# Four edits to the state-space layer of a four-layer kernel on one core

## The chip, the cores and the metric

## The reference

The input is x, 8 sequences of 512 tokens with 256 features. The change touches the third layer alone:

```python
xp = x @ Wx.T                       # 512 columns: 64 heads of 8
Bm = rmsnorm((x @ WB.T).reshape(B_, L, H, N), Bn_w) + B_bias     # H = 64, N = 128
Cm = rmsnorm((x @ WC.T).reshape(B_, L, H, N), Cn_w) + C_bias
dt = softplus(x @ Wdt.T);  lam = sigmoid(x @ Wlam.T)
theta_cumsum = cumsum((x @ Wth.T).reshape(B_, L, H, N // 2) * dt[..., None], axis=1)
Bm, Cm = rope(Bm, theta_cumsum), rope(Cm, theta_cumsum)
alpha = exp(-dt * exp(A_log));  beta = (1 - lam) * dt * alpha;  gamma = lam * dt
# over the tokens, per head:
h = alpha * h + beta * outer(B_prev, x_prev) + gamma * outer(B, x)
y = C @ h
```

with x normalised before it, and `y * silu(z) @ Wout.T` behind it.

## The kernel before, in words

Each layer is a row of phases; a phase is a function with a block of its own, in which the five queues (SP for transfers, TensorE, ScalarE, VectorE, GpSimd) run lists written out by hand and wait for each other on counted semaphores. A barrier parts the phases. Products in full precision are done as three fp32r matmuls over a high and a low part (`matmul3`, L45; its lines L48 to L50), for each of two blocks of 128 features, so a 128x512 product is six matmuls.

Three phases matter here. `gates` (L870) computes dt, lam and the decays: TensorE's eight products `ga_z`, ScalarE's Sigmoid, Abs, Exp, Ln (L946 to L952), a long row of 128x2048 operations on VectorE, two more Exp (L954 on `tmp`, L956 for the growths), and twelve groups of transpositions whose copies (L962) go to DRAM as `token_gates`. `input_projection` (L1003) computes xp in 32 tiles of 128 tokens: six matmuls, a copy by ScalarE (L1065), a store by SP (L1025); VectorE first copies each tile's x_hi and x_lo into a staging buffer.

`state_space` (L1182) is the long one. Its work is 256 turns, 32 pairs of heads times 8 sequences, two turns (j = 0, 1) to a loop iteration. A turn takes a sequence of 512 tokens as four chunks (TPB) of 128 tokens. Within a chunk the recurrence is a masked product (scores times decay), between chunks it is a state carried by sums. Turn k projects, normalises and rotates B and C of unit k, while scores, sums and outputs are made for the units before it. TensorE's list (`turn`, L1497) is:

- half of B (`p_b[1]`), the angle of the next unit (into `p_sum`), `outputs` (L1432 over the states, L1438 over the masked scores), the other half of B, `exponents` (L1447, L1449: decay exponents into the score banks `p_se`)
- half of C, `turn_b` e = 0 (three transpositions, L1461, into `p_c[0]`, and the growth rows spread by four small matmuls, L1464), `squares` 0 (the sum of B's squares over a head, L1495, into `p_sum`, which the angle has just left), the other half of C
- `turn_b` e = 1 into `p_m`, `scores` (L1476), `chunk_sums` (L1485: `bt`, 128 columns, is the loaded side, `xe`, 16 columns, the moving one), `squares` 1 (the sum of C's squares)

ScalarE squares the projections (L1573, L1580), takes exponents (`decays`, L1553), copies the transposed B (L1559), makes 1/sqrt as Ln and Exp (L1564, L1566) and the sines (`angles`, L1545 to L1549). Ln and Exp need another function table than Sin, so each turn has two table loads. VectorE runs `phases` (L1607 to L1612: dt times angle, running sum, fraction `fr`), `combine` (L1616, L1617), `rotate` for B (L1624 to L1629), `states` with `masked` (L1634 to L1646) and `rotate` for C. GpSimd adds squares and halves of the rotation, splits the next weights (L1380, L1382), adds the diagonal to the decays (L1363, L1367) and scales xp (L1394, L1396). SP loads, per turn, one weight chunk, the growth and decay rows (`load_rows`) and dt rows spread over 64 partitions each (`load_dt`, L1259).

What orders a turn around the change, on TensorE:

```python
def squares(k, q):
    pe.wait_ge((ss_b, ss_c)[q], k + 1)
    if q == 0:
        pe.wait_ge(fr_done, k + 2)
    else:
        pe.wait_ge(ln_b, k + 1)
    M(p_sum[:], pairs_sum[:], sq[:, q, 0], start=True, stop=True).then_inc((sum_b, sum_c)[q], 1)
```

## Time and profile before

| | |
|---|---|
| median of 3 runs | 6169.8 us (6169.16 to 6174.46) |
| the profiled execution | 6162.61 us, its span 6160.8 us |
| TensorE busy | 5549.1 us (90%) |
| VectorE busy | 4509.5 us (73%) |
| GpSimd busy | 3636.6 us (59%) |
| ScalarE busy | 3505.7 us (57%) |
| mean granted tensor clock | 0.945 |

Busy times are shares of the whole span; the phases have different limits, so they are only a first look. A timeline row gives the start, the duration, the engine, the line, the tiles written and read, the count of merged instructions, and in brackets the idle time before it with what ended it. TensorE's durations run until a matmul's last result is out, so they overlap; what a group costs TensorE is read from its start to the next group's start.

### The profile page before, as it was taken

To read this page: it belongs to the slowest core of one execution; us is meant where nothing else is said; L and a number is where in the kernel's file an instruction comes from. 1 tells how busy PE (TensorE), PEld (TensorE's weight loads), DVE (VectorE), ACT (ScalarE), POOL (GpSimd) and SP (SyncE) were. 2 spreads that over 40 slices of the span, in tenths; PEclk is the share of its full clock that TensorE was granted. 3 is DMA by queue.
4 is the path that set the end of the run, shared out by engine and by line. 5 is a ranking of instruction groups with operands and counts; after the bars stand their busy time and mean duration, and the time that the engine had idled before them with its cause. 6 is when DMAs were issued, how large, how long until landed. Compare 5 with 4: busy or idle time off the path is not lost. (4 is left out here: it accounts for less than half of the span.)

```text
span 6160.8 us, 127971 instructions
## 1 busy us (share of the span) xinstructions
PE 5549.1 (90%) x40796; PEld 3972.6 (64%) x40796; DVE 4509.5 (73%) x6856; ACT 3505.7 (57%) x4756; POOL 3636.6 (59%) x4101
## 2 busy tenths in 40 slices
PE   5999588459999999999999999999999999984699
PEld 3454277337777777777777777777777777763587
DVE  5777555538888888888888888888888888835444
ACT  2444222227777777777777777777777777731222
POOL 2222000018888888888888888888888888820000
PEclk9889599679999999999999999999999999986799
DMA  3333200131111111111111111111111111121100
GB/s 100 108 114 118 79 18 24 38 121 32 29 29 30 28 34 29 29 29 30 32 28 31 29 32 29 29 31 27 34 29 29 29 30 32 28 90 62 42 24 20
DMA packets 435078, 267.89 MB, mean 43 GB/s; under 512 B 269092, under 2 KB 363876, under 8 KB 434052
## 3 DMA queue, kind: packets, MB, share of 16 engines
q1 hardware_dynamic: 417284, 257.14, 15.1%
q10 hardware_dynamic: 17664, 9.44, 0.5%
q14 instruction: 101, 0.83, 0.0%
q8 instruction: 29, 0.48, 0.0%
HBM read 186.73 MB, written 66.85 MB: 41 GB/s over the span
## 5 line engine op out<-in xcount | busy, mean ns | idle before, releaser
L1564 ACT ACTIVATE ss_r<-ss_pssum,ss_eps 128x512 f32<-128x512 f32 x512 | 352.9, 689 | 901.8 <-PE ss_pssum L1495 901.8
L1624 DVE SCALAR_TENSOR_TENSOR ss_psb<-ss_psb,ss_norm,ss_r 128x512 f32<-128x512 f32 x512 | 362.9, 754 | 446.4 <-ACT ss_r L1566 446.4
L1495 PE MATMUL ss_pssum<-ss_sq,ss_pairssum 128*128 128x512 f32 x1024 | 570.9, 639 | 57.7 <-DVE ss_fr L1612 57.7
L1376 POOL TENSOR_TENSOR ss_sq<-ss_sq 128x512 f32<-128x512 f32 x256 | 329.6, 1287 | 451.6 <-ACT ss_sq L1573 451.6
L48 PE MATMUL ss_psb<-x_hi,ss_whi 128*128 x1024 | 529.5, 517 | 4.4 <-DVE ss_fr L1612 4.4
L1476 PE MATMUL ss_psse<-ss_rot 64*128 64x128 f32 x8224 | 530.0, 279 | 0.3 <-POOL ss_rot L1358 0.3
L1406 POOL TENSOR_TENSOR ss_own<-ident,ss_tk 128x512 f32<-128x512 f32 x512 | 524.4, 1045 | 0.0
L1476 PEld LDWEIGHTS ss_psse<-ss_rot 64*128 64x128 f32 x8224 | 480.6, 188 | 43.6 <-issue 43.0
L48 PE MATMUL ss_psc<-x_hi,ss_whi 128*128 x1024 | 506.6, 495 | 0.0
L1366 POOL TENSOR_TENSOR ss_sq<-ss_sq 128x512 f32<-128x512 f32 x256 | 325.1, 1270 | 136.0 <-ACT ss_sq L1580 136.0
L50 PE MATMUL ss_psb<-x_hi,ss_wlo 128*128 x1024 | 403.7, 394 | 0.0
L49 PE MATMUL ss_psc<-x_lo,ss_whi 128*128 x1024 | 403.6, 394 | 0.0
L50 PE MATMUL ss_psc<-x_hi,ss_wlo 128*128 x1024 | 402.3, 393 | 0.0
L49 PE MATMUL ss_psb<-x_lo,ss_whi 128*128 x1024 | 401.8, 392 | 0.0
L1485 PE MATMUL ss_psm<-ss_xe,ss_bt 128*128 128x16 f32 x3084 | 388.8, 264 | 0.0
L1331 POOL MEMSET ss_rot<- 128x4096 f32 x1 | 3.5, 3512 | 652.3 <-POOLq L2045 652.3
L1485 PEld LDWEIGHTS ss_psm<-ss_xe,ss_bt 128*128 128x128 f32 x3084 | 363.8, 191 | 31.3 <-issue 0.2
L1624 DVE SCALAR_TENSOR_TENSOR ss_psc<-ss_psc,ss_norm,ss_r 128x512 f32<-128x512 f32 x512 | 361.7, 752 | 0.0
L1646 DVE TENSOR_TENSOR ss_gm<-ss_psse,ss_dec 128x1024 f32<-128x1024 f32 x257 | 314.7, 1225 | 41.7 <-POOL ss_dec L1367 41.7
L1566 ACT ACTIVATE ss_r<-ss_r 128x512 f32<-128x512 f32 x512 | 324.6, 634 | 16.3
L1400 POOL TENSOR_TENSOR ss_rot<-ss_rot,ss_tmp 128x512 f32<-128x512 f32 x256 | 332.8, 1300 | 0.0
L1546 ACT ACT_TABLE_LOAD x257 | 329.7, 1283 | 4.6
(346 smaller groups left out, 15582.3 us busy)
## 6 DMA issues: line engine op xcount, KB each, us to landing
ss_dtb<-time_steps SPq DMA_DIRECT2D x516, 128.0 KB, 2.9
ss_wraw<-in_w_state SPq DMA_DIRECT2D x264, 80.0 KB, 2.3
head_rows<-a_yhi SPq DMA_DIRECT2D x64, 256.0 KB, 2.5
a_qs<-head_rows SPq DMA_DIRECT2D x128, 96.0 KB, 2.2
a_ks<-head_rows SPq DMA_DIRECT2D x128, 96.0 KB, 2.2
ss_xp<-x_heads SPq DMA_DIRECT2D x33, 256.0 KB, 4.2
y_heads<-ss_yo SPq DMA_DIRECT2D x132, 64.0 KB, 2.4
head_rows<-a_ylo SPq DMA_DIRECT2D x32, 256.0 KB, 2.7
```

The lines of the kernel that those rows point to most:

```text
L48: nc.tensor.matmul(out, w_hi, x_hi, start=first, stop=False)
L49: nc.tensor.matmul(out, w_hi, x_lo, start=False, stop=False)
L50: return nc.tensor.matmul(out, w_lo, x_hi, start=False, stop=last)
L1376: G.tensor_tensor(sq[:, 0, 0], sq[:, 0, 0], sq[:, 0, 1], ALU.add).then_inc(ss_b, 1)
L1400: G.tensor_tensor(rot[:, j, 0], rot[:, j, 0], tmp[:, 0, 0], ALU.add)
L1406: last = G.tensor_tensor(own[:, h * TPB:(h + 1) * TPB], g.ident[:].rearrange("p (o t) -> p o t", o=1).broadcast_to([P, TPB, P]), at_diagon ...
L1476: last = M(p_se[:, h * TPB + c, :], rot[at, 1 - j, e, cols], rot[at, 1 - j, 2 + e, cols], start=e == 0, stop=e == 1)
L1485: last = M(p_m[:, (c * 2 + e) * PW:(c * 2 + e + 1) * PW], bt[:, 2 if e else j, c, :], xe[:, 1 - j, c, :], start=True, stop=True)
L1495: M(p_sum[:], pairs_sum[:], sq[:, q, 0], start=True, stop=True).then_inc((sum_b, sum_c)[q], 1)
L1546: A(trig[:, j, 0], fr[:], ACT.Sin, scale=UNDER_TURN)
L1564: A(r[:, q], p_sum[:], ACT.Ln, scale=1.0 / N1, bias=eps[:, 0:1]).then_inc(ln, 1)
L1624: link.mark(S(bank[:, e, :], bank[:, e, :], norm[:, 2 * q + e:2 * q + e + 1], r[:, q], ALU.mult, ALU.mult))
```

## The change

Five things are done, in two phases:

1. B ahead of the angle. TensorE's list has both halves of B first, then the angle, the outputs, B's transpositions, C's first half, B's sum, and C's second half split around the exponents.
2. B's sum and its first transpositions go to the score banks (`first_half` and `second` of `p_se`) instead of `p_sum` and `p_c[0]`. The B sum no longer waits for `fr_done`, C's second half no longer waits for the copy of the transpositions; the exponents now wait for that copy and for `ln_b`. ScalarE's list follows: two of the four angle operations before Square of B, two behind it, the B copy and B norms ahead of the decays, Square of C ahead of the second copy.
3. Chunk sums' sides exchanged. `xe` (widened by zeros to 32 columns) is loaded, `bt` (128 columns) moves, the three chunks go to three strips of 32 partitions; VectorE masks the result into `sums` (96x128), one transposition (`turn_sums`) brings it back. The state copy (L1636 before) comes behind the masked scores.
4. Growth rows by transfer. Four DMAs a turn spread them over 4 x 16 partitions; the four small matmuls and their part of the copy go.
5. One gates stage. `input_projection` is gone; its 32 products, copies and stores are part of `gates_and_heads`, the copies at four places of ScalarE's list. The staging copies are gone, and four PSUM banks instead of two hold tiles.

```diff
@@ gates -> gates_and_heads
+            sp.wait_ge(w_split, 2)
+            sp.dma_start(x_raw, wx_d).then_inc(loaded, 16)
+            for t in range(TILES):
+                sp.wait_ge(x_taken, t + 1)
+                sp.dma_start(xp_v[t], heads[:, t % 2]).then_inc(x_out[t % 2], 16)
             sp.wait_ge(rows_ready, 1)
...
+            pe.wait_ge(x_split, 2)
+            for t in range(TILES):
+                if t >= 4:
+                    pe.wait_ge(x_taken, t - 3)
...
+            def take_heads(t):
+                act.wait_ge(x_done, t + 1)
+                if t >= 2:
+                    act.wait_ge(x_out[t % 2], 16 * (t // 2))
+                A(heads[:, t % 2], px[t % 4][:], ACT.Copy).then_inc(x_taken, 1)
...
             A(dt[:], z[:], ACT.Abs).then_inc(act_sem, 1)
+            take_heads(0)
             A(ea[:], ea[:], ACT.Exp).then_inc(act_sem, 1)
             act.wait_ge(act_sem, 3)
             A(dt[:], dt[:], ACT.Exp, scale=-1.0).then_inc(act_sem, 1)
+            take_heads(1)
             act.wait_ge(act_sem, 4)
             A(dt[:], dt[:], ACT.Ln, bias=1.0).then_inc(act_sem, 1)
+            for t in range(2, TILES // 2):
+                take_heads(t)
             act.wait_ge(dve_to_act, 1)
             A(tmp[:], tmp[:], ACT.Exp).then_inc(act_sem, 1)
+            for t in range(TILES // 2, TILES):
+                take_heads(t)
@@ state_space, SP
-                sp.dma_start(grown[:, j, :], grown_dram[ds(j * H1 + pair * 2, 2), ds(i * SEQ, SEQ)]).then_inc(rows_in[j], 16)
...
+            def load_growth(pair, i, j):
+                for c in range(TPB):
+                    source = grown_dram[ds(j * H1 + pair * 2, 2), ds(i * SEQ + c * P, P)].rearrange("h (o t) -> h o t", o=1)
+                    sp.dma_start(grown[32 * c:32 * c + PW, j, :], source.broadcast_to([2, P1, P])).then_inc(growth_in[j], 16)
...
-                    sp.wait_ge(turned[0], u)
+                    sp.wait_ge(e_done, u)
                     load_rows(pair, i, j)
+                    latest = (u + UNITS - 1) % UNITS
+                    sp.wait_ge(y_ready, u)
+                    load_growth(latest // BATCH, (latest // 2) % (BATCH // 2), 1 - j)
                     sp.wait_ge(thdt_done, u + 1)
@@ state_space, TensorE
-                for c in range(3):
-                    for e in range(2):
-                        last = M(p_m[:, (c * 2 + e) * PW:(c * 2 + e + 1) * PW], bt[:, 2 if e else j, c, :], xe[:, 1 - j, c, :],
-                                 start=True, stop=True)
+                for e in range(2):
+                    for c in range(3):
+                        last = M(p_m[32 * c:32 * c + 32, 3 * P:4 * P], xe[:, 1 - j, c, (1 - e) * PW:(3 - e) * PW],
+                                 bt[:, 2 if e else j, c, :], start=e == 0, stop=e == 1)
                 last.then_inc(u_done, 1)
+
+            def turn_sums(k):
+                pe.wait_ge(um_done, k + 1)
+                T(p_m[:, 0:6 * PW], sums[:], g.ident[0:96, 0:96]).then_inc(ut_done, 1)
...
                 half(p_b[:, 1, :], 2, wpar, b)
+                half(p_b[:, 0, :], 1, wpar, b).then_inc(b_done, 1)
                 pe.wait_ge(ln_c, k)
                 pe.wait_ge(wt_in, (k + 1) // BATCH * 32 + 32)
                 project(p_sum[:], wt_hi, wt_lo, (k + 1) % BATCH).then_inc(th_done, 1)
                 outputs(k, j)
-                half(p_b[:, 0, :], 1, wpar, b).then_inc(b_done, 1)
-                exponents(k, j, (n + j) * 80)
+                turn_b(k, j, 0)
                 pe.wait_ge(rope_c, k)
                 half(p_c[:, 1, :], 4, wpar, b)
-                turn_b(k, j, 0)
                 squares(k, 0)
-                pe.wait_ge(taken[0], k + 1)
-                half(p_c[:, 0, :], 3, wpar, b).then_inc(c_done, 1)
+                half(p_c[:, 0, :], 3, wpar, b, [0])
+                pe.wait_ge(ln_b, k + 1)
+                exponents(k, j, (n + j) * 64)
+                half(p_c[:, 0, :], 3, wpar, b, [1]).then_inc(c_done, 1)
                 turn_b(k, j, 1)
                 scores(k, j)
                 chunk_sums(k, j)
                 squares(k, 1)
+                turn_sums(k)
@@ state_space, ScalarE
-            angles(1, 0)
             with act.Fori(0, UNITS // 2) as n:
                 for j in range(2):
                     k = n * 2 + j
+                    half_angles(k + 1, j)
                     act.wait_ge(b_done, k + 1)
                     A(sq[:, 0], p_b[:], ACT.Square).then_inc(sq_b, 1)
+                    other_angles(k + 1, j)
                     nc.scalar.preload_act_table_set("natural_log_exp_and_others")
-                    decays(k)
                     take_b(k, j, 0)
                     norms(k, 0)
-                    take_b(k, j, 1)
+                    decays(k)
                     act.wait_ge(c_done, k + 1)
                     A(sq[:, 1], p_c[:], ACT.Square).then_inc(sq_c, 1)
+                    take_b(k, j, 1)
                     norms(k, 1)
-                    angles(k + 2, 1 - j)
@@ state_space, VectorE (states)
-                link(V.tensor_tensor(sums, sums, blocks[:].rearrange("p (o d) -> p o d", o=1).broadcast_to([P, 6, PW]), ALU.mult))
+                V.tensor_tensor(sums[:], p_m[0:96, 3 * P:4 * P], block_rows[:], ALU.mult).then_inc(um_done, 1)
                 entering = lambda c: state[:, c, :, 0:PW]
-                link.mark(V.tensor_copy(entering(1), added[:, 0]))
-                moved = link.n
                 masked(k)
-                link.wait(moved)
+                dve.wait_ge(ut_done, k + 1)
+                link(V.tensor_copy(entering(1), added[:, 0]))
```

How the lists come out. On TensorE, the middle of a turn before, from the exponents to the B sum (`ss_psse` the score banks, `ss_psc` and `ss_psb` the products of C and B, `ss_pssum` the sum bank):

```order
L1447 MATMUL ss_psse<-ss_strict,ident 128x512 x2
L1449 MATMUL ss_psse<-ss_right,ss_left 128x512 x2
L48 MATMUL ss_psc<-x_hi,ss_whi 128x512
L49 MATMUL ss_psc<-x_lo,ss_whi 128x512
L50 MATMUL ss_psc<-x_hi,ss_wlo 128x512
L48 MATMUL ss_psc<-x_hi,ss_whi 128x512
L49 MATMUL ss_psc<-x_lo,ss_whi 128x512
L50 MATMUL ss_psc<-x_hi,ss_wlo 128x512
L1461 MATMUL ss_psc<-ident,ss_rot 128x128 x3
L1464 MATMUL ss_psc<-ss_grown,ss_heads 32x128 x4
L1492 REGISTER_ALU
L1495 MATMUL ss_pssum<-ss_sq,ss_pairssum 128x512
```

and in the changed kernel, from the B sum to the second transpositions:

```order
L1483 MATMUL ss_psse<-ss_sq,ss_pairssum 128x512
L48 MATMUL ss_psc<-x_hi,ss_whi 128x512
L49 MATMUL ss_psc<-x_lo,ss_whi 128x512
L50 MATMUL ss_psc<-x_hi,ss_wlo 128x512
L1433 REGISTER_ALU
L1437 MATMUL ss_psse<-ss_strict,ident 128x512 x2
L1439 MATMUL ss_psse<-ss_right,ss_left 128x512 x2
L48 MATMUL ss_psc<-x_hi,ss_whi 128x512
L49 MATMUL ss_psc<-x_lo,ss_whi 128x512
L50 MATMUL ss_psc<-x_hi,ss_wlo 128x512
L1451 MATMUL ss_psm<-ident,ss_rot 128x128 x3
```

The exponents have moved from before C's first half to the middle of its second, behind the B sum, and the growth matmuls are gone.

On ScalarE, the head of the loop body before, then of the changed kernel (the ISA row opens the body in both):

```order
L1569 ISA
L1573 ACTIVATE ss_sq<-ss_psb 128x1024
L1574 ACT_TABLE_LOAD
L1553 ACTIVATE ss_dec<-ss_psse 128x1024
L1559 ACTIVATE ss_bt<-ss_psc 128x512
L1564 ACTIVATE ss_r<-ss_pssum,ss_eps 128x512
L1566 ACTIVATE ss_r<-ss_r 128x512
```

```order
L1560 ISA
L1536 ACT_TABLE_LOAD
L1536 ACTIVATE ss_trig<-ss_fr 128x512
L1537 ACT_TABLE_LOAD
L1537 ACTIVATE ss_trig<-ss_fr 128x512
L1565 ACTIVATE ss_sq<-ss_psb 128x1024
L1540 ACTIVATE ss_trig<-ss_fr 128x512
L1542 ACTIVATE ss_trig<-ss_trig,ss_quarter 128x512
L1567 ACT_TABLE_LOAD
L1551 ACTIVATE ss_bt<-ss_psse 128x384
L1556 ACTIVATE ss_r<-ss_psse,ss_eps 128x512
L1558 ACTIVATE ss_r<-ss_r 128x512
```

Abs now opens the body, with a table load ahead of it that stands in the first of the two turns only; the decays' exp has moved behind the B norms.

## Rows read from the trace of the kernel before

**Rows 1.** Busy time by engine in one turn: us, busy (instructions), clock, DMA share, GB/s
```profile
3003.07:3018.87 15.80, 15.63 (x130) 11.22 (x129) 13.23 (x20) 11.45 (x15) 13.45 (x16) 1.00 0.08 23
```

**Rows 2.** Timeline of TensorE in that turn: start us, duration us, engine, line, operation
```profile
3006.33 0.65 PE L1432 MATMUL ss_psm<-ss_rot,ss_state 128*32 128x128 f32 x16
3006.79 0.62 PE L1438 MATMUL ss_psm<-ss_gm,ss_xk 128*32 128x128 f32 x16
...
3008.84 0.61 PE L1447 MATMUL ss_psse<-ss_strict,ident 128*128 128x512 bf16 x2
3009.38 0.39 PE L1449 MATMUL ss_psse<-ss_right,ss_left 15*128 15x512 bf16 x2
3009.69 0.50 PE L48 MATMUL ss_psc<-x_hi,ss_whi 128*128 x1
...
3011.21 0.49 PE L1461 MATMUL ss_psc<-ident,ss_rot 128*128 128x128 f32 x3
3011.63 0.42 PE L1464 MATMUL ss_psc<-ss_grown,ss_heads 2*32 2x128 f32 x8
3012.22 1.12 PE L1495 MATMUL ss_pssum<-ss_sq,ss_pairssum 128*128 128x512 f32 x2 [0.17 <-DVE ss_fr L1612]
...
3016.97 1.51 PE L1485 MATMUL ss_psm<-ss_xe,ss_bt 128*128 128x16 f32 x12
3018.33 1.10 PE L1495 MATMUL ss_pssum<-ss_sq,ss_pairssum 128*128 128x512 f32 x2
```

**Rows 3.** Timeline of VectorE in that turn
```profile
3003.02 0.19 DVE L1636 COPY ss_state<-ss_psm 128x32 f32<-128x32 f32 x1
3003.37 1.23 DVE L1646 TENSOR_TENSOR ss_gm<-ss_psse,ss_dec 128x1024 f32<-128x1024 f32 x1 [0.17 <-POOL ss_dec L1367]
...
3005.07 1.41 DVE L1624 SCALAR_TENSOR_TENSOR ss_psc<-ss_psc,ss_norm,ss_r 128x512 f32<-128x512 f32 x2
...
3007.58 1.28 DVE L1629 SCALAR_TENSOR_TENSOR ss_tmp<-ss_psc,ss_bias,ss_trig 128x1024 f32<-128x1024 f32 x1
```

**Rows 4.** Timeline of GpSimd in that turn
```profile
3016.57 1.27 POOL L1366 TENSOR_TENSOR ss_sq<-ss_sq 128x512 f32<-128x512 f32 x1 [0.48 <-ACT ss_sq L1580]
3017.80 1.26 POOL L1367 TENSOR_TENSOR ss_dec<-ss_dec,ss_own 128x512 f32<-128x512 f32 x1
```

**Rows 5.** Timeline of ScalarE in that turn
```profile
3003.67 0.69 ACT L1564 ACTIVATE ss_r<-ss_pssum,ss_eps 128x512 f32<-128x512 f32 x1 [2.98 <-PE ss_pssum L1495]
...
3004.93 0.61 ACT L1545 ACTIVATE ss_trig<-ss_fr 128x512 f32<-128x512 f32 x1
...
3009.03 1.02 ACT L1573 ACTIVATE ss_sq<-ss_psb 128x1024 f32<-128x1024 f32 x1 [0.41 <-PE ss_psb L50]
3010.07 1.28 ACT L1574 ACT_TABLE_LOAD   x1
3011.37 1.02 ACT L1553 ACTIVATE ss_dec<-ss_psse 128x1024 f32<-128x1024 f32 x1
3012.29 0.59 ACT L1559 ACTIVATE ss_bt<-ss_psc 128x512 f32<-128x512 f32 x1
3013.39 0.69 ACT L1564 ACTIVATE ss_r<-ss_pssum,ss_eps 128x512 f32<-128x512 f32 x1 [0.51 <-PE ss_pssum L1495]
```

**Rows 6.** Timeline of SP's queue in that turn: issue of the dt rows
```profile
3014.49 1.54 SPq L1259 DMA_DIRECT2D ss_dtb<-time_steps  x2
```

**Rows 7.** Timeline of `gates`, `input_projection` and the start of `state_space`
```profile
1224.18 1.91 ACT L954 ACTIVATE ga_tmp<-ga_tmp 128x2048 f32<-128x2048 f32 x1 [16.02 <-DVE ga_tmp L989]
...
1245.11 1.91 ACT L956 ACTIVATE ga_lam<-ga_cum 128x2048 f32<-128x2048 f32 x1 [19.01 <-DVE ga_keep L996]
...
1273.42 0.34 SPq L1020 DMA_DIRECT2D xp_raw<-in_w_x  x1
...
1284.36 44.86 SPq L1025 DMA_DIRECT2D x_heads<-xp_outt  x32
...
1331.79 0.34 SPq L1241 DMA_DIRECT2D ss_norm<-in_state_norm  x1
```

More of the change, by code:

```diff
@@ L891, in gates @@
         pt = [ps(f"t{i}", [P, 4, P]) for i in range(2)]
+        px = [ps(f"x{i}", [P, DIN]) for i in range(4)]
+        xp_v = xp_dram.rearrange("(n p) d -> n p d", p=P)
         block = mem.enter_context(nc.Block())
@@ L910, in _ @@
             sp.wait_ge(stored, 112)
+            for p in range(2):
+                sp.wait_ge(x_out[p], 16 * (TILES // 2))
         @block.tensor
@@ L924, in _ @@
                 last.then_inc(z_done, 1)
+            pe.wait_ge(x_split, 2)
+            for t in range(TILES):
+                if t >= 4:
+                    pe.wait_ge(x_taken, t - 3)
+                tok = slice(t * P, (t + 1) * P)
+                for k in range(KD):
+                    last = matmul3(nc, px[t % 4][:], g.x_hi[:, k, tok], g.x_lo[:, k, tok], x_whi[:, k], x_wlo[:, k],
+                                   k == 0, k == KD - 1)
+                last.then_inc(x_done, 1)
             for n in range(12):
@@ L1193, in state_space @@
     taken = [sem("taken0"), sem("taken1")]
[L1194 to L1195 removed]
+    y_ready, thdt_done, fr_done, rope_b, rope_c, um_done, s_ready, gm_done, chain_sem = (
+        sem(n) for n in ("yready", "thdt", "fr", "ropeb", "ropec", "um", "sready", "gm", "chain"))
     ss_b, ss_c, rot_b, rot_c, dd_done, xk_done, own_done, pool_chain = (
@@ L1228, in state_space @@
         p_sum, p_m = ps("sum", [P, SEQ]), ps("m", [P, SEQ])
+        first_half, second = (p_se[:, h * TPB:(h + 1) * TPB, :].rearrange("p c t -> p (c t)") for h in range(2))
+        sums_of = (first_half, p_sum[:])
         added = p_m[:, 0:6 * PW].rearrange("p (c e d) -> p c e d", e=2, d=PW)
@@ L1415, in _, with project @@
             M, T = nc.tensor.matmul, nc.tensor.transpose
-            def project(out, hi, lo, b):
-                for q in range(KD):
+            def project(out, hi, lo, b, parts=range(KD)):
+                for q in parts:
                     tok = ds(b * SEQ, SEQ)
@@ L1453, in turn_b @@
             def turn_b(k, j, e):
-                bank = p_m[:] if e else p_c[:, 0, :]
+                bank = p_m[:] if e else second
                 if e:
@@ L1461, in turn_b @@
                     last = T(bank[:, c * P:(c + 1) * P], rot[:, 1 - j, e, c * P:(c + 1) * P], g.ident[:])
-                if e == 0:
-                    for c in range(TPB):
-                        last = M(bank[32 * c:32 * c + 32, 3 * P:4 * P], heads[:], grown[:, 1 - j, c * P:(c + 1) * P],
-                                 start=True, stop=True)
                 last.then_inc(turned[e], 1)
@@ L2062, in program @@
         with phase(nc):
-            gates(nc, ctx, i["w_dt"], i["a_log"], tk, dt, grown, decay, ends, g)
-        with phase(nc):
-            input_projection(nc, ctx, i["w_x"], xp, g)
+            gates_and_heads(nc, ctx, i["w_dt"], i["a_log"], i["w_x"], xp, tk, dt, grown, decay, ends, g)
         with phase(nc):
             state_space(nc, ctx, i["w_state"], i["state_norm"], i["state_bias"], i["left"], i["right"], i["strict"],
-                        i["blocks"], i["heads"], tk, dt, grown, decay, ends, xp, y, g)
+                        i["blocks"], i["block_rows"], tk, dt, grown, decay, ends, xp, y, g)
         with phase(nc):
```

142 lines of the change are left out of this document (46 added, 96 removed).

## The prediction

> **What bounds the kernel now.** First the page: TensorE is busy 90% of the span and the state-space turn holds most of its work. 256 turns (32 pairs of heads times 8 sequences of 512 tokens, two turns per loop iteration) run at one rhythm, so one turn read instruction by instruction is the profile that matters. The window of one turn [rows 1] is 15.80 us long; TensorE is busy 15.63 of it at a granted clock of 1.00, VectorE 13.23, GpSimd 13.45, ScalarE 11.45. Then TensorE's timeline inside the turn [rows 2]: its groups start where the group before lets them, and only the B sum (L1495) shows a wait, 0.17 us for `fr`. So **the turn is TensorE's list of work, with hardly a hole in it**; taking work off TensorE shortens the turn, until VectorE, GpSimd or a ring through several engines takes over. Third, the timelines of VectorE, GpSimd and ScalarE [rows 3 to 5] give the lengths of such a ring. All times below are against the profiled execution, 6162.6 us (span 6160.8); the median of the three runs, 6169.8, is 7.2 higher, and I add that at the end.
>
> **TensorE's list after the change.**
> - Gone: the four growth matmuls behind the B transposes, L1464 at 3011.63 to the next start at 3012.22 [rows 2], **0.59 us** (that includes the wait for `fr`: the B sum now has its own bank and no longer needs it).
> - Chunk sums: today 3016.97 to 3018.33, **1.36 us** for twelve passes (six fp32 matmuls) that load 128 columns of weights for 16 moving columns. The exchange makes the 32 columns of `xe` the weights and lets 128 columns move, into three 32-row strips. The nearest row is L1432, the same 128*32 form: sixteen passes over four strips from 3006.33 to 3006.79, 0.46 us [rows 2]. Twelve over three strips have the same four rounds, so **0.46 us**. Bounds: 0.35 (at the sixteen's pace) and 1.68, if strips take turns (twelve at the 0.14 of a full 128x128 transposition, below).
> - New: one transposition of the masked sums. Three take 0.42 us (3011.21 to 3011.63 [rows 2]), so 0.14, plus a hand-over of 0.10: **0.24** (bounds 0.14 and 0.42).
> - The first C product is split by the exponents: one more hand-over, **0.10**, between nothing and the 0.17 us hole at L1495.
> - List: 15.80 - 0.59 - 1.36 + 0.46 + 0.24 + 0.10 = **14.65 us**.
>
> What the Trainium skill says of the exchange cuts both ways. "TensorE: Matmul & The Clock Gate", Part 3 (Packing small matmuls), states that a weight load runs beside a matmul in flight only if their row groups differ; the three strips share theirs, so by it the loads would be added. L1432's row, whose strips share a row group too, speaks against it: sixteen passes in 0.46 us leave no room for sixteen loads in series. With loads added (the page's figure gives 27 ns per 32 columns, an estimate of 0.32 us for twelve), the list would be 14.97.
>
> **Why the turn does not become 14.65.** The change puts the exponents behind the B sum's logarithm (`ln_b`), because the sum now lives in their bank, and the decays' exp behind the B norms on ScalarE. What hung loosely today is now one ring: C product 1, B sum, logarithm, exponents, exp, three GpSimd additions, mask, states, rotation of C, and back to C product 1, which waits `rope_c`. From rows: product 1.52 (3009.69 to 3011.21) + B sum to logarithm 1.17 (3012.22 on TensorE to 3013.39 on ScalarE) + logarithm 0.69 and 0.05 hand-over + exponents 0.93 (3008.84 to 3009.38 + 0.39) [rows 2, 5] + hand-over 0.08 + exp 1.02 + hand-over 0.08 + additions 1.26, 1.23, 1.26 with 0.10 behind them [rows 4] + mask and two state steps 1.70 (3003.37 to 3005.07) + the state copy, today ahead of the mask and now behind it, 0.30 (between its own 0.19 and the 0.35 from its start at 3003.02 to the mask's) + rotation 3.79 (3005.07 to 7.58 + 1.28) [rows 3] + 0.05 = **15.23 us**. TensorE's own holes come out alike: three matmuls of C cover only part of the logarithm (0.2 to 0.3), the scores wait for the exp (0.1), the C sum for GpSimd (0.1): 14.65 + 0.5 = 15.1. I take 15.23. Part of the gain on TensorE's list is thus given back.
>
> **A table load that the diff does not show.** ScalarE's order has one more ACT_TABLE_LOAD, ahead of Abs at the head of the loop body, so in every second turn; today's loop opens with Square and has none there. Its price is 1.28 us [rows 5]. In that turn ScalarE runs without a hole from the C sum to the B logarithm: C sum to its logarithm 1.14 (3018.33 to 3003.67 + 15.80) + logarithm and exp 1.26 (to Abs at 3004.93) + load 1.30 + Abs, load and three Sines 3.69 (3004.93 to 3009.03 - 0.41) + Square and load 2.34 (3009.03 to 3011.37) + B copy 0.40 (under the 0.59 of its four-chunk form) + logarithm 0.74 = 10.87. From the exponents on: 0.93 + 0.08 + 1.02 + 0.08 + 1.26 + 1.23 + 0.08 to the C sum again = 4.68. Together **15.55 us** in this turn; without the load 14.25, below the ring. The mean turn is (15.55 + 15.23) / 2 = **15.39**, a gain of 0.41 us; 256 turns give **105 us**.
>
> **Costed at nothing.** The four growth loads per turn go through SP's queue ahead of the dt rows. The nearest row is the dt pair, 1.54 us of issue for two broadcasts [rows 6]; four such are 3.1 in a turn of 15. They are issued when one turn's combine is done and read by the combine two turns on; were that cover gone, VectorE would wait at the combine and the 3.1 would show. VectorE's list keeps its length: the mask of the sums is 96x128 where it was 128x96, and the combine multiplies by `grown` instead of `bt`. It loses its wait for the B norms and becomes nearly full, but stays under 15. GpSimd writes as many elements as before. The dt, decay and weight loads keep a turn of lead.
>
> **The gates stage.** input_projection disappears: from its first load at 1273.42 to state_space's first at 1331.79, **58.4 us** [rows 7]. Its 32 tiles move into gates, where TensorE stands idle while ScalarE and VectorE work, but the tiles' copies now sit in ScalarE's list. Two stand ahead of Ln and delay the rest by 2 x 0.59 = 1.2 (a 128x512 copy out of PSUM lasts 0.59 [rows 5]). The other 30 come at the pace of the stores, 44.86 / 32 = 1.40 us each [rows 7], 42.0 in all; ScalarE is idle 16.02 + 19.01 = 35.0 in the two gaps they fill. What overflows, 7.0, and the 1.2 push the growth exp, and all behind it: **8.2 us**. Net **50 us** (57 if the copies fit the gaps, 32 if a tile takes 2 us). The weights' split on VectorE lies under its long idle wait for Ln.
>
> **Sum.** 6162.6 - 105 - 50 = 6007.6; with the 7.2, **6015 us**, 2.5% less than the median. About 0.2% is what a measurement of this kernel can tell from no change.
>
> **Rivals.**
> - The added table load is absorbed (another piece of ScalarE's chain turns out shorter, or the logarithm waits anyway): 15.23 in every turn, 256 x 0.57 = 146; 5974 us. For it: the two results lie 0.32 apart, less than the chain's errors could add.
> - The rings are looser than I sum them and TensorE's 14.65 alone decides, with 0.1 of holes: 256 x 1.05 = 269 and 50; 5851 us. Against it: each hand-over in the ring is a wait in order, and VectorE and GpSimd have 13.2 and 13.5 of their own.
> - Loads of the chunk sums are not hidden. A load of 128 columns costs at most 1.36 / 12 = 0.11, a quarter of it 0.03, twelve 0.34: sums 0.80. From the exponents to the C sum TensorE then needs 0.85 + 0.76 + 0.41 + 1.99 + 0.80, 0.13 more than GpSimd's leg; 6048 us. This is the price of the skill's rule named above, in rows.
> - **Slower: the strips do not run side by side.** Then the sums cost 1.68, that leg is 5.69 instead of 4.68, the turn with the load 16.56 and the other 14.65 + 1.22 + 0.3 = 16.17: mean 16.37, 256 x 0.57 = +146, less 50: 6266 us. It decides from sums of about 1.3 us, where the mean turn passes 16.0 (15.80 + 50 / 256). Against it stands L1432, whose sixteen would last 2.2 us in turns and last 0.46.
> - The stages joined bring nothing (the tiles' stores or copies hold up the gates by all they saved): 6065 us.
>
> **Chances.** Forecast 0.50, absorbed load 0.15, looser rings 0.10, unhidden loads 0.10, joined stages worthless 0.07, strips in turn 0.08. The range, 5930 to 6085, takes in the forecast with its bounds, the first, third and fifth case. Faster by over 0.2%: 0.90; within 0.2%: 0.03; slower: 0.07, the strips.
>
> **What would show it.** In the profile after: turns that alternate, about 15.55 and 15.2 us; chunk sums at 0.46 us between their start and the C sum's; a hole on TensorE ahead of the exponents, longer (0.5) in the turn with two table loads before Square, 0.2 in the other; GpSimd waiting for the exp of the decays, over 1 us a turn, where it waited for Square; VectorE's wait for the B norms at L1624 down to some 0.4 or less and instead a wait of 0.9 for GpSimd at the mask; no wait at the combine for the growth rows; from gates' start to state_space's some 50 us less. Wrong it would be if all turns are alike, if TensorE stays without holes, or if a queue (SP) shows up as a releaser.

## The result: 6095 us, faster by 1.2%, and the profile after

| | before | after |
|---|---|---|
| median of 4 runs, us | 6172.1 | **6095.4** (6093.36 to 6105.01) |
| ratio, 95% interval | | 0.988 (0.9864 to 0.9896) |
| profiled execution, us (span) | 6162.6 (6160.8) | 6105.0 (6103.2) |
| one state-space turn, mean of 255 | 15.853 | 15.784 |

The forecast was 6015, the range 5930 to 6085. The sign was right; the gain is 77 us where 155 were forecast, and the time lies outside the range. In the profiled execution of the changed kernel the two layers ahead of `gates` take some 12.5 us more (its first load at 1177.30, before at 1164.75). The change doesn't touch them, and in the traces of the experiments below, whose first two layers are the same, that load lies anywhere from 1167.73 (`woven`) to 1176.32 (`growth_back`). So parts are compared by their own windows here.

The **gates stage** from its first load to `state_space`'s first, on SP's queue:

```profile
1177.30 0.34 SPq L903 DMA_DIRECT2D ga_raw<-in_w_dt  x1
...
1212.90 52.51 SPq L909 DMA_DIRECT2D x_heads<-ga_heads  x32
...
1289.62 0.34 SPq L1221 DMA_DIRECT2D ss_norm<-in_state_norm  x1
```

It lasts 1289.62 - 1177.30 = 112.3 us; before, the two phases took 1331.79 [rows 7] less 1164.75, 167.0. Gain 54.7, forecast 50. Of the 77 us that arrived, most came from here.

**All turns**, from the first square of B to the last (busy time by engine as in [rows 1]):

```profile
1331.30:5356.30 4025.00, 3787.03 (x30860) 2605.21 (x30859) 3370.48 (x4843) 3022.43 (x3953) 3425.64 (x3824) 1.00 0.13 32
```

4025.00 / 255 = 15.784 a turn (255 turns from the first square to the 256th); TensorE is busy 3787.03 of the 4025.00. The same window of the kernel before:

```profile
1376.20:5418.80 4042.60, 3985.05 (x32642) 2855.54 (x32640) 3375.64 (x4844) 2918.65 (x3826) 3430.33 (x3825) 1.00 0.13 30
```

Of TensorE's 3985.05 busy us 198 did go, but only 18 us of time went with them: 180 became waits.

Where they stand, **TensorE's timeline** in one turn says:

```profile
3006.94 0.50 PE L48 MATMUL ss_psc<-x_hi,ss_whi 128*128 x1 [0.26 <-DVE ss_tmp L1622]
...
3008.43 1.02 PE L1483 MATMUL ss_psse<-ss_sq,ss_pairssum 128*128 128x512 f32 x2
...
3010.49 0.59 PE L1437 MATMUL ss_psse<-ss_strict,ident 128*128 128x512 bf16 x2 [0.35 <-ACT ss_r L1556]
...
3014.59 0.64 PE L1471 MATMUL ss_psm<-ss_bt,ss_xe 128*32 128x128 f32 x12
3015.18 1.12 PE L1483 MATMUL ss_pssum<-ss_sq,ss_pairssum 128*128 128x512 f32 x2
3016.14 0.25 PE L1477 MATMUL ss_psm<-ident,ss_sums 96*128 96x96 f32 x1
...
3022.79 0.50 PE L48 MATMUL ss_psc<-x_hi,ss_whi 128*128 x1 [0.78 <-DVE ss_tmp L1622]
```

The chunk sums take 0.59 (3014.59 to 3015.18) where they took 1.36 [rows 2]. But the C product (first and last line, 15.85 apart) waits for VectorE's rotation, and the exponents wait for the logarithm. The waits are those of the forecast's ring: work that goes from engine to engine and comes back to where it began, so that no turn can be shorter than it. So a ring decides, as forecast. Its pieces on **VectorE** from the decay mask to the rotation, on **GpSimd** at its first addition, and on **ScalarE** from one C logarithm to the next, in this order:

```profile
3016.38 1.22 DVE L1637 TENSOR_TENSOR ss_gm<-ss_psse,ss_dec 128x1024 f32<-128x1024 f32 x1 [0.80 <-POOL ss_dec L1356]
3017.52 0.18 DVE L1630 COPY ss_state<-ss_psm 128x32 f32<-128x32 f32 x1
3018.39 0.25 DVE L1631 SCALAR_TENSOR_TENSOR ss_state<-ss_state,ss_ends,ss_psm 128x32 f32<-128x32 f32 x1 [0.69 <-DVE ss_state L1630]
3018.79 0.25 DVE L1632 SCALAR_TENSOR_TENSOR ss_state<-ss_state,ss_ends,ss_psm 128x32 f32<-128x32 f32 x1 [0.15 <-DVE ss_state L1631]
3018.95 1.41 DVE L1617 SCALAR_TENSOR_TENSOR ss_psc<-ss_psc,ss_norm,ss_r 128x512 f32<-128x512 f32 x2
```
```profile
3012.54 1.27 POOL L1352 TENSOR_TENSOR ss_dec<-ss_dec,ss_own 128x512 f32<-128x512 f32 x1 [1.01 <-ACT ss_dec L1546]
```
```profile
3000.57 0.69 ACT L1556 ACTIVATE ss_r<-ss_pssum,ss_eps 128x512 f32<-128x512 f32 x1 [2.57 <-PE ss_pssum L1483]
...
3001.95 1.28 ACT L1536 ACT_TABLE_LOAD   x1
...
3003.89 1.28 ACT L1537 ACT_TABLE_LOAD   x1
...
3009.56 0.68 ACT L1556 ACTIVATE ss_r<-ss_psse,ss_eps 128x512 f32<-128x512 f32 x1
...
3011.44 1.03 ACT L1546 ACTIVATE ss_dec<-ss_psse 128x1024 f32<-128x1024 f32 x1 [0.54 <-PE ss_psse L1439]
...
3016.34 0.69 ACT L1556 ACTIVATE ss_r<-ss_pssum,ss_eps 128x512 f32<-128x512 f32 x1 [2.58 <-PE ss_pssum L1483]
```

Read as a **ring** from C product to C product, the forecast's terms beside what is measured:

| piece | forecast | measured |
|---|---|---|
| C product to B sum; B sum to logarithm | 1.52 + 1.17 | 1.49 + 1.13 |
| logarithm's start to exponents | 0.74 | **0.93** (3009.56 to 3010.49) |
| exponents to exp; exp to GpSimd | 1.01 + 1.10 | 0.95 + 1.10 |
| GpSimd's three additions to the mask | 3.85 | 3.84 (3012.54 to 3016.38) |
| mask, copy, two state steps | 2.00 | **2.57** (3016.38 to 3018.95) |
| rotation of C to C product | 3.84 | 3.84 (3018.95 to 3022.79) |
| sum | 15.23 | 15.85 |

Two terms are short by 0.19 and 0.57. (The C product before this pair started at 2991.22, so that turn is 15.72 long; in it the first state step comes 0.79 behind the copy, where it is 0.87 here.) A **second ring** is nearly as long: in the turn whose Abs needs a table load, ScalarE has no hole from the C logarithm to the B one. C sum to C logarithm 1.16 (2999.41 to 3000.57) + C logarithm to B logarithm 8.99 (to 3009.56) + to the exponents 0.93 + to the next C sum 4.69 (3010.49 to 3015.18) = 15.77. It was forecast as 15.55; the 0.19 is missing there too.

### The profile page after: what moved, and what is told of

Read it like the earlier page. It is cut to its first block and busy times, and to the rows that moved or that the text cites. A ratio compares the mean times of both kernels' runs of the same rounds, so it can differ in the third digit from the quotient of the medians.

```text
span 6103.2 us, 126388 instructions
## 1 busy us (share of the span) xinstructions
PE 5363.7 (88%) x38997; PEld 3728.5 (61%) x38997; DVE 4488.7 (74%) x6792; ACT 3604.7 (59%) x4878; POOL 3631.8 (60%) x4101
## 3 DMA queue, kind: packets, MB, share of 16 engines
q1 hardware_dynamic: 434872, 264.57, 15.6%
## 5 line engine op out<-in xcount | busy, mean ns | idle before, releaser
L48 PE MATMUL ss_psc<-x_hi,ss_whi 128*128 x1024 | 559.9, 547 | 133.5 <-DVE ss_tmp L1622 133.5
L1556 ACT ACTIVATE ss_r<-ss_pssum,ss_eps 128x512 f32<-128x512 f32 x256 | 176.2, 688 | 660.5 <-PE ss_pssum L1483 660.5
L1352 POOL TENSOR_TENSOR ss_dec<-ss_dec,ss_own 128x512 f32<-128x512 f32 x257 | 327.9, 1276 | 393.0 <-ACT ss_dec L1546 393.0
L48 PE MATMUL ss_psb<-x_hi,ss_whi 128*128 x1024 | 425.7, 416 | 28.9 <-issue 17.6
L1365 POOL TENSOR_TENSOR ss_sq<-ss_sq 128x512 f32<-128x512 f32 x256 | 328.4, 1283 | 160.3 <-ACT ss_sq L1565 160.3
L48 PEld LDWEIGHTS ss_psc<-x_hi,ss_whi 128*128 128x128 f32 x1024 | 191.7, 187 | 324.0 <-DVE ss_tmp L1622 193.1
L1546 ACT ACTIVATE ss_dec<-ss_psse 128x1024 f32<-128x1024 f32 x257 | 263.7, 1026 | 141.1 <-PE ss_psse L1439 141.1
L1346 POOL TENSOR_TENSOR ss_rot<-ss_rot,ss_tmp 128x512 f32<-128x512 f32 x257 | 330.3, 1285 | 20.3 <-DVE ss_tmp L1622 8.5
L1390 POOL TENSOR_TENSOR ss_rot<-ss_rot,ss_tmp 128x512 f32<-128x512 f32 x256 | 332.1, 1297 | 0.0
```

Of the source, the lines that this page charges most:

```text
L48: nc.tensor.matmul(out, w_hi, x_hi, start=first, stop=False)
L1346: G.tensor_tensor(rot[:, 1 - j, 2], rot[:, 1 - j, 2], tmp[:, 1, 0], ALU.add)
L1352: G.tensor_tensor(dec[:, 0:TPB], dec[:, 0:TPB], own[:, 0:TPB], ALU.add)
L1365: G.tensor_tensor(sq[:, 0, 0], sq[:, 0, 0], sq[:, 0, 1], ALU.add).then_inc(ss_b, 1)
L1390: G.tensor_tensor(rot[:, j, 0], rot[:, j, 0], tmp[:, 0, 0], ALU.add)
```

## The experiments

Times are medians of four runs (five for the kernel with the old sides), each batch beside seven or eight runs of the kernel before; in those its median lay between 6170.4 and 6173.1.

**Gates alone** (`gates_only`). The kernel before, with `gates_and_heads` in place of the two phases and nothing else.

```diff
-            gates(nc, ctx, i["w_dt"], i["a_log"], tk, dt, grown, decay, ends, g)
-        with phase(nc):
-            input_projection(nc, ctx, i["w_x"], xp, g)
+            gates_and_heads(nc, ctx, i["w_dt"], i["a_log"], i["w_x"], xp, tk, dt, grown, decay, ends, g)
```

> The kernel before with the joined gates stage alone, state_space as it was. The trace of the change puts the time from the first load of gates to the first of state_space at 112.3 us where it was 167.0. Theory: the two parts add, and this one is worth 55 us: 6117 us. Rival (the joined stage gives some of it back in state_space, for instance by a later start of its loads): under 40 us, over 6130. Were the turns the main part of the gain: under 20 us.

6117.2 us, ratio 0.991 (0.9895 to 0.9928): 54 us less than before; in its trace the joined stage takes 112.0 us, as in the change. The state-space edits together are thus worth 6117.2 - 6095.4 = 22 us.

**State copy ahead of the mask** (`copy_first`).

```diff
-                masked(k)
                 dve.wait_ge(ut_done, k + 1)
-                link(V.tensor_copy(entering(1), added[:, 0]))
+                link.mark(V.tensor_copy(entering(1), added[:, 0]))
+                moved = link.n
+                masked(k)
+                link.wait(moved)
```

> The change with the state copy put back ahead of the masked scores (it waits for the turned sums there). In the trace of the change the copy starts behind the mask and the next state step starts 0.87 us after it, 0.69 of that idle on VectorE. Theory (a ring through rotation of C, C product 1, B sum, exponents, exp, GpSimd, mask and states sets the turn): the ring gets shorter by 0.87 less what the copy costs ahead of the mask (0.2 to 0.4), so 0.5 us a turn, 120 us in all, 5975 us. Rival (the table load ahead of Abs sets every second turn and TensorE's list the other): no gain beyond 20 us. Second rival (the idle 0.69 is a transfer or a register step that just moves along): within 15 us of the change.

6008.0, ratio 0.974 (0.9721 to 0.9753), 87 less than the change, where 120 were expected. The ring was the bound. VectorE's timeline of this kernel, from the mask to the scaling of C:

```profile
3017.47 0.19 DVE L1629 COPY ss_state<-ss_psm 128x32 f32<-128x32 f32 x1 [0.84 <-PE ss_psm L1477]
3017.58 1.21 DVE L1639 TENSOR_TENSOR ss_gm<-ss_psse,ss_dec 128x1024 f32<-128x1024 f32 x1
3018.71 0.24 DVE L1633 SCALAR_TENSOR_TENSOR ss_state<-ss_state,ss_ends,ss_psm 128x32 f32<-128x32 f32 x1
3019.10 0.25 DVE L1634 SCALAR_TENSOR_TENSOR ss_state<-ss_state,ss_ends,ss_psm 128x32 f32<-128x32 f32 x1 [0.15 <-DVE ss_state L1633]
3019.26 1.41 DVE L1617 SCALAR_TENSOR_TENSOR ss_psc<-ss_psc,ss_norm,ss_r 128x512 f32<-128x512 f32 x2
```

From the mask to the scaling it is 1.68 (3017.58 to 3019.26) where the change had 2.57: the first state step follows the mask without idle time, the second keeps its 0.39. Why the gain is not more, ScalarE's timeline says, by the starts of the C logarithm:

```profile
3002.32 0.69 ACT L1556 ACTIVATE ss_r<-ss_pssum,ss_eps 128x512 f32<-128x512 f32 x1 [2.58 <-PE ss_pssum L1483]
...
3017.38 0.69 ACT L1556 ACTIVATE ss_r<-ss_pssum,ss_eps 128x512 f32<-128x512 f32 x1 [2.58 <-PE ss_pssum L1483]
...
3033.16 0.69 ACT L1556 ACTIVATE ss_r<-ss_pssum,ss_eps 128x512 f32<-128x512 f32 x1 [2.58 <-PE ss_pssum L1483]
```

The turns now alternate: 15.06 without the extra load, 15.78 with it. The second is the ScalarE ring of 15.77 above, which this edit does not touch.

**One table load less** (`one_load`): the Sine table, which has Abs too, is loaded ahead of Abs, so that Abs needs none of its own; four loads to a loop body.

```diff
+                if j == 0:
+                    nc.scalar.preload_act_table(ACT.Sin)
                 act.wait_ge(fr_done, count)
                 A(trig[:, j, 1], fr[:], ACT.Abs).then_inc(abs_done, 1)
```

> The change with the sine's table asked for ahead of Abs in the first turn of the loop body, so that Abs runs with it and the body has four table loads instead of five. Theory (the ring through VectorE sets both turns, since both are 15.8 us long): ScalarE gets 1.3 us back in every second turn and nobody waits for it there, gain under 10 us. Rival, the one of my forecast (the extra load costs 0.32 us a turn on average): 128 x 0.6 or so, 40 to 80 us, 6020 to 6055 us.

6095.3 (6088.8 to 6096.4), no difference. The forecast's price for this load (0.32 us in every second turn) is refuted for this kernel. Without the load ScalarE waits 1.26 us for the B sum ahead of the B logarithm, in the turn where the change had no idle time there.

**The exponents' waits** (`exp_waits`): the wait for the decay rows goes ahead of the three matmuls of C that come before the exponents; the wait for the B copy is dropped, since the logarithm, which stands behind it on ScalarE, implies it.

```diff
-                pe.wait_ge(rows_in[1 - j], loads)
-                pe.wait_ge(taken[0], k + 1)
 ...
+                pe.wait_ge(rows_in[1 - j], (n + j) * 64)
                 half(p_c[:, 0, :], 3, wpar, b, [0])
                 pe.wait_ge(ln_b, k + 1)
```

> The change with the exponents' wait for the decay rows taken ahead of C's second product and their wait for the B copy dropped as implied by ln_b (ScalarE copies before it takes the logarithm). In the trace of the change TensorE starts the exponents 0.25 to 0.28 us after the logarithm's end, where such hand-overs elsewhere take 0.05. Theory (the register step and waits behind ln_b sit on the ring): 0.2 us a turn, about 50 us. Rival (the delay is the logarithm's own semaphore or the ring is not the bound): under 15 us.

6053.4, ratio 0.981 (0.9791 to 0.9824), 42 less than the change; the mean turn of the two traces differs by 0.18 us. ScalarE's timeline, from the B logarithm to the decays' exp:

```profile
3018.21 0.68 ACT L1557 ACTIVATE ss_r<-ss_psse,ss_eps 128x512 f32<-128x512 f32 x1
...
3019.92 1.03 ACT L1547 ACTIVATE ss_dec<-ss_psse 128x1024 f32<-128x1024 f32 x1 [0.36 <-PE ss_psse L1437]
```

They are 1.71 apart, in the change 1.88 (3009.56 to 3011.44). The B copy stands ahead of the logarithm in ScalarE's list, and the decay rows' wait costs nothing where it was moved to, so both had been met. Two met waits cost this much where they stand behind the one that comes last; which of the two costs it was not tried.

**Both edits** (`copy_exp`), and **all three** (`all3`), by the same edits.

> The change with both edits that helped: state copy ahead of the mask (-87 us alone) and the exponents' two implied waits moved or dropped (-42 alone); five table loads per loop body stay. If both shorten one and the same ring, their gains add: 6095 - 129 = 5966. If after the copy's edit ScalarE's chain (the turn with the extra load) is what the turn waits for, the second edit still takes 0.16 from it, but the load's 1.28 us now shows: 5980 to 6000. I take 5980.

> The same with four table loads in place of five. In the change itself the fifth load cost nothing (6095.3 against 6095.4). Theory: it cost nothing only because the ring through the exponents was longer than ScalarE's chain. With the ring 0.5 us shorter it must cost something: 15 to 50 us faster than the kernel with the two edits, that is 5935 to 5965. Rival: ScalarE's chain never decides in this kernel; then both kernels agree within 5 us.

5960.4 (0.966) and 5888.6 (0.9539, 0.9523 to 0.9555). The first is 20 under the number taken and 6 under the plain sum of the two gains, so these two edits add up. The load that cost 0 in the change costs 72 us here, more than the 15 to 50 that were expected. ScalarE's timeline with both edits and five loads, then with four:

```profile
3012.76 0.69 ACT L1557 ACTIVATE ss_r<-ss_pssum,ss_eps 128x512 f32<-128x512 f32 x1 [2.58 <-PE ss_pssum L1481]
...
3027.66 0.69 ACT L1557 ACTIVATE ss_r<-ss_pssum,ss_eps 128x512 f32<-128x512 f32 x1 [2.57 <-PE ss_pssum L1481]
```
```profile
3013.01 0.69 ACT L1559 ACTIVATE ss_r<-ss_pssum,ss_eps 128x512 f32<-128x512 f32 x1 [2.58 <-PE ss_pssum L1481]
...
3027.89 0.69 ACT L1559 ACTIVATE ss_r<-ss_pssum,ss_eps 128x512 f32<-128x512 f32 x1 [2.58 <-PE ss_pssum L1481]
```

The turns without the extra load are 14.90 and 14.88, alike. With five loads the other turn is 15.6 (the C logarithm before the first line starts at 2997.16), which is the ring of 15.77 less the 0.19; with four, the mean of all turns is 14.95. The three edits bring 87, 42 and 0 us singly and 207 together: 87 and 42 add to 135, and the load's 72 come on top. "ScalarE: Activation LUTs", section "What ACT_TABLE_LOAD costs", of the Trainium skill puts a switch at 1.28 us for the load and 1.38 more for a drain. From these figures 128 loads would be 340 us, an estimate. The trace agrees on the 1.28, but shows no drain beside it: the load starts 0.02 behind the operation before (3003.24 + 0.63 to 3003.89 in the change's trace) and the next operation 0.01 behind the load (3003.89 + 1.28 to 3005.18). What the 128 loads cost the kernel went from 0 to 72 us with what stood around them.

**Sides undone** (`old_sides`): the chunk sums as before, with their mask on VectorE and the copy ahead of the mask, no transposition.

```diff
-                for e in range(2):
-                    for c in range(3):
-                        last = M(p_m[32 * c:32 * c + 32, 3 * P:4 * P], xe[:, 1 - j, c, (1 - e) * PW:(3 - e) * PW],
-                                 bt[:, 2 if e else j, c, :], start=e == 0, stop=e == 1)
+                for c in range(3):
+                    for e in range(2):
+                        last = M(p_m[:, (c * 2 + e) * PW:(c * 2 + e + 1) * PW], bt[:, 2 if e else j, c, :],
+                                 xe[:, 1 - j, c, PW:2 * PW], start=True, stop=True)
 ...
```

> The change with the chunk sums' sides as they were before: six matmuls with 128 columns of weights and 16 moving, masked on VectorE, the copy ahead of the mask, no transposition. TensorE's list grows by 0.75 - 0.25 = 0.5 us a turn; the ring loses the 0.57 us that the copy costs behind the mask. If the ring decides (the theory), this is faster than the change, about as far as the kernel with the copy first: 6010 to 6050, I take 6030. If TensorE's list decides, as the exchange of sides assumes, it is slower than the change by 0.5 x 256 = 128: 6223.

6149.3, ratio 0.996 (0.9949 to 0.9977), 54 slower than the change: neither number. ScalarE's C logarithms show why:

```profile
3003.17 0.69 ACT L1550 ACTIVATE ss_r<-ss_pssum,ss_eps 128x512 f32<-128x512 f32 x1 [3.34 <-PE ss_pssum L1479]
...
3018.57 0.69 ACT L1550 ACTIVATE ss_r<-ss_pssum,ss_eps 128x512 f32<-128x512 f32 x1 [3.34 <-PE ss_pssum L1479]
...
3035.09 0.69 ACT L1550 ACTIVATE ss_r<-ss_pssum,ss_eps 128x512 f32<-128x512 f32 x1 [3.33 <-PE ss_pssum L1479]
```

The turn without the extra load did fall, to 15.40. The other rose to 16.52, the ScalarE ring (15.77) with 0.77 for the longer sums (1.36 for 0.59), which lie between exponents and C sum. The expectation had looked at one ring and not at the other.

**Sides undone, with the edits of the loads and the waits** (`old_sides3`; its copy stands ahead of the mask too).

> The chunk sums' sides as before, now with four table loads and the exponents' waits moved. With the sides alone undone the turn with the fifth load grew to 16.5 us: theory, that was ScalarE's chain, C sum to B logarithm with two table loads, pushed 0.77 us later by the longer sums. With four loads that is gone and TensorE's list decides: sums 1.36 in place of 0.59, no transposition and its 0.45 behind the C sum, net 0.32 x 256 = 82 us over 5889, that is 5971. Rival: the longer sums hit the ring whatever ScalarE loads; then the 54 us between the change and this edit alone stay on top of the two edits' gain: 6020 or more.

5958.0, 69 over the kernel with the three edits: near the theory's 82, and not the rival's 131 or more. So the sides' exchange is worth 69 us in this surrounding. The exchange takes more than that off TensorE's list (0.77 a turn in the sums, less the new transposition), but part of it becomes a wait for the rotation of C. TensorE's timeline, from the B transpositions to the C product, in `all3` and then in this kernel:

```profile
3018.13 0.55 PE L1449 MATMUL ss_psse<-ident,ss_rot 128*128 128x128 f32 x3
3018.72 0.50 PE L48 MATMUL ss_psc<-x_hi,ss_whi 128*128 x1
```
```profile
3019.62 0.55 PE L1449 MATMUL ss_psse<-ident,ss_rot 128*128 128x128 f32 x3
3019.93 0.48 PE L48 MATMUL ss_psc<-x_hi,ss_whi 128*128 x1
```

The C product starts 0.59 behind the transpositions in `all3`, 0.06 after VectorE's rotation has ended (3017.39 + 1.27), and 0.31 behind them with the old sides, where nothing holds it up.

**State steps woven into C's scalings** (`woven`; `woven3` with the loads' and waits' edits too): mask, copy, scale 0, state step, scale 1, state step.

```diff
-                link(S(entering(2), entering(1), ends[:, ds(at + 1, 1)], added[:, 1], ALU.mult, ALU.add))
-                S(entering(3), entering(2), ends[:, ds(at + 2, 1)], added[:, 2], ALU.mult, ALU.add).then_inc(s_ready, 1)
+                return second_state, third_state
 ...
+                scaled_0 = scaled(0)
+                if between:
+                    between[0]()
+                    reached = link.n
+                scaled(1)
+                if between:
+                    between[1](reached)
```

> The change with the two state steps woven between the two scalings of C (mask, copy, scale 0, state step, scale 1, state step), so that each step's chain wait and register step run beside 0.6 us of other work. The ring loses the same 0.57 us as with the copy first, up to 0.7, and VectorE no longer waits 0.84 us for the transposition ahead of the mask. Theory: what bounds next is the logarithm ahead of the exponents, so 5990 to 6010, I take 6000. Rival: that wait of VectorE was the bound of the kernel with the copy first; then up to 0.3 us a turn more goes, 5930.

> The kernel with all three edits, with the state steps woven into C's scalings in place of the copy ahead of the mask. In the kernel with the three edits TensorE has hardly a hole (turn 14.87 us), and VectorE waits 0.85 for the transposition, which nobody behind it feels. Theory: TensorE's list decides, so the way in which the copy is hidden no longer matters: 5888 within 10. Rival: VectorE's 0.85 still reaches C product 1; then the woven order gains up to 0.3 us a turn, 5810.

5997.0 and **5877.5** (ratio 0.9524, 0.9508 to 0.954), the fastest of all: 3.6% under the change. The woven order removes no work. It is 11 us faster than the copy ahead of the mask, both times (6008.0 and 5888.6): VectorE's wait of 0.85 ahead of the copy mattered no more than that. The theory had allowed 10 for `woven3`.

**Four small matmuls put back** (`growth_back` in the change, `growth_back3` in the kernel with three edits), behind the B transposes where the growth matmuls were.

```diff
+                if e == 0:
+                    for c in range(TPB):
+                        last = M(bank[32 * c:32 * c + 32, 3 * P:4 * P], g.ident[0:2, 0:32], g.ident[0:2, :], start=True, stop=True)
                 last.then_inc(turned[e], 1)
```

> The change with four small matmuls behind the B transposes again (two rows by 32 columns, 128 moving, as the growth matmuls were, on constants), 0.42 us of TensorE's time a turn at the place where they stood. Theory: a ring decides and TensorE waits 0.26 and 0.78 us for the rotation of C right behind this place, so the four go into the hole: 0 to 15 us, 6100. Rival (TensorE's list decides): 0.42 x 256 = 108, 6203.

> The same four matmuls in the kernel with all three edits, whose TensorE has hardly a hole. Theory: here they cost their full 0.42 us x 256 = 108: 5997. If something else than TensorE's list sets its turn of 14.87 us, they cost less than 30: 5915.

6108.5 and 5979.6: the same work costs 13 us in the change and 91 in the kernel with the three edits, where TensorE has less idle time; 108 were expected there. TensorE's timeline of the second, the same 0.42 us of matmuls as in [rows 2]:

```profile
3014.59 0.55 PE L1449 MATMUL ss_psse<-ident,ss_rot 128*128 128x128 f32 x3
3015.06 0.42 PE L1452 MATMUL ss_psse<-ident 2*32 2x128 f32 x8
3015.41 0.50 PE L48 MATMUL ss_psc<-x_hi,ss_whi 128*128 x1
```

From the transpositions to the C product it is 0.82 here, 0.51 more than where nothing holds the product up (0.31). Where it would have waited for the rotation anyway (0.59), the four cost 0.23; so the 91 us, 0.36 a turn, are a mean of turns of both kinds.

**What the 0.69 is** (`static_ends`): the state steps read their decay from a fixed column of ones, not from a column whose place a register holds. The states then don't decay.

```diff
-                link(S(entering(2), entering(1), ends[:, ds(at + 1, 1)], added[:, 1], ALU.mult, ALU.add))
-                S(entering(3), entering(2), ends[:, ds(at + 2, 1)], added[:, 2], ALU.mult, ALU.add).then_inc(s_ready, 1)
+                link(S(entering(2), entering(1), ones[:, 1:2], added[:, 1], ALU.mult, ALU.add))
+                S(entering(3), entering(2), ones[:, 2:3], added[:, 2], ALU.mult, ALU.add).then_inc(s_ready, 1)
```

> The change with the decay of the two state steps read from a constant column of ones instead of a column addressed by a register (the states then do not decay; nothing else is left out). Theory: of the 0.87 us from the copy to the first state step, 0.15 is the chain wait (as between the two steps) and the rest, 0.5, is VectorE's queue working out the address of that column behind the wait. Then the idle time of 0.69 ahead of the first step falls to 0.15 or so, the ring shortens by 0.5, and the kernel lands near the one with the copy first: 6000 to 6020. Rival: the 0.69 is the price of a small copy right behind the big product, whatever is addressed; then 6095.

5999.5, ratio 0.9721 (0.9705 to 0.9737), 96 less than the change. VectorE's timeline, for the same three lines as in the change:

```profile
3004.02 0.18 DVE L1630 COPY ss_state<-ss_psm 128x32 f32<-128x32 f32 x1
3004.23 0.25 DVE L1631 SCALAR_TENSOR_TENSOR ss_state<-ss_state,ss_ones,ss_psm 128x32 f32<-128x32 f32 x1
3004.52 0.25 DVE L1632 SCALAR_TENSOR_TENSOR ss_state<-ss_state,ss_ones,ss_psm 128x32 f32<-128x32 f32 x1
```

Copy to step is 0.21, not 0.87, and step to step 0.29, not 0.40. So 0.66 + 0.11 = 0.77 us of that turn is what the two register-held places cost (0.58 + 0.11 in the turns where copy to step was 0.79). That it is VectorE's queue working the places out behind the wait is the reading that fits; the trace shows only the idle time that went. (The turns came out at 15.03 and 15.77: as with the copy first, the one with the extra load stays at ScalarE's ring, so the gain is 0.37 a turn and not 0.77.) The rival (the price of a small copy behind the product) is refuted.

## Why the prediction was right in sign and short in size

- **The gates stage: right.** 50 forecast, 54.7 in the trace, 54 alone on the chip.
- **TensorE's list: not the bound, as forecast, but summed some 0.3 too long.** Forecast 14.65 us; no turn of the changed kernel shows it bare. In `all3` a turn of 14.88 holds a wait of 0.26 for the logarithm and one of 0.28 for the rotation of C (0.59 less 0.31), so the list alone is about 14.3, an estimate from these rows. In `old_sides3` only the 0.26 is left, and its turns are 15.22 all through. Chunk sums 0.46 forecast, 0.59 measured. The row that was taken for them (L1432) has another group of its own form behind it; L1438's sixteen have a full-width matmul behind them, as the sums do, and take 0.55 (3006.79 to 3007.34). It is no wait for GpSimd's addition: in the few turns of `all3` where that ended earlier (sums at 1486.80, addition over at 1486.95, C sum at 1487.37) the sums still take 0.57. The rule of the Trainium skill ("TensorE: Matmul & The Clock Gate", Part 3, Packing small matmuls), that a weight load overlaps matmuls in flight only when their row groups differ, gave the prediction's estimate of 0.78 (0.46 and 0.32 for the loads). The measured 0.59 lies below it, and no run here parts loads from passes. The growth matmuls were put at 0.59 with a wait in it; put back, four such cost 0.51 of list (`growth_back3`).
- **That a ring decides instead: right**, and shown from both sides: 0.42 us of TensorE's work put back costs 0.05 a turn (13 / 256), and hiding the idle time ahead of the first state step, without removing work, gains 87 us (`copy_first`), and hiding it ahead of both gains 98 (`woven`).
- **The step that failed is one term of that ring:** "the state copy, today ahead of the mask and now behind it, 0.30", bounded by its own 0.19 and the 0.35 from its start to the mask's. Mask, copy and steps measured 2.57 against 2.00. In these 2.57 the copy's term, from its start to the first state step, is 0.87 (3017.52 to 3018.39; 0.79 in the turn beside it) against 0.30; mask to copy (1.14) and the two steps (0.40 and 0.16) are what they were in the 1.70. Both bounds were taken from rows in which the mask stood behind the copy [rows 3] and hid what follows it: the wait for the copy and the register-held place of the state step's decay. Taking the mask out from between exposed that, 0.66 us of it by `static_ends`. The second step's 0.11 was in the rows before too (step to step 0.39), so it is no part of the miss. The 0.35 was the price of the copy under cover, not the price of what the cover hid.
- **A smaller term failed in the same way:** "logarithm 0.69 and 0.05 hand-over" left out that the exponents have two more waits behind the logarithm's: 0.93 measured against 0.74. That is 0.19 of the ring, and 42 us by `exp_waits`.
- Together 0.76 short, less 0.14 by which other terms were long: 15.85 against 15.23. Of the 0.41 a turn that was forecast, 0.07 was left. That is the miss: 105 - 18 = 87 us in the turns, of which the gates gave 5 back; the median lies 80 over the forecast.
- **The table load: the rival had its price right (nothing) and the turn wrong.** By the forecast the load was to lengthen its turn by 0.32. It cost nothing, since the other ring was not 15.23 in every turn, as the rival's 5974 us had it, but a mean 15.78, as long as the 15.77 of this one. ScalarE's chain itself was summed well: 10.87 forecast from C sum to the end of the B logarithm with a hand-over of 0.05 in it, 10.83 measured without one (2999.41 to 3010.24). `all3` shows that the load bites (72 us) as soon as the other ring is shorter.
- **What would show it:** as forecast, GpSimd's wait for the exp is over 1 us (1.01 and 2.09), VectorE's at the mask 0.80, and there is no wait for growth rows. Not as forecast, the hole ahead of the exponents is alike in both turns (0.35 and 0.33, where 0.5 and 0.2 were named), and so are the turns: 15.77 and 15.80 from C logarithm to C logarithm, not 15.55 and 15.2. The prediction had named that as a sign of being wrong, and it was one. In `copy_first` they do alternate.
- The rival on the slow side (strips one after the other, 6266) is excluded by the 0.59.

## What to carry to other kernels

Before an instruction is moved out from between two others, look at what its duration hid: a wait, and above all a register-addressed operand of the next instruction, whose price shows in no row while it is covered. In a ring, put the wait that comes last alone and directly ahead of its work, and those met earlier ahead of it. With two rings of nearly equal length an edit to one alone can show nothing (the load: 0 us by itself, 72 once the other ring was 135 us shorter), so a null result for one part does not say that the part is free: its worth is read again once the other ring is cut.

## What was not expected of the hardware

Two register-addressed operands cost VectorE 0.77 us in a turn when they stand bare behind a wait, 0.66 for the first and 0.11 for the second. The first costs nothing where the mask of 1.2 us runs over it (`copy_first`), and neither shows idle time where a scaling of 0.75 us does (`woven`). The rows show the price as idle time put down to the instruction before (0.69, "<-DVE ss_state L1630"), which reads like a slow copy. Two met waits of TensorE's queue cost 0.18 us a turn behind the one that comes last. Which part of the first price is arithmetic on registers and which is the instruction's own set-up was not tried.
